# A four-block attention kernel on one core: all of the key spread by transfers, padded query features, and new orders

## The reference, cut to what matters

```python
attn  = softmax(q @ k.T * D**-0.5)                 # block 3, per head
attn2 = softmax(gate * attn)
out   = (w * attn2 + (1 - w) * attn) @ v @ w_proj + b_proj
```

## Time and profile before

| | before |
|---|---|
| median of 3 runs | 479.83 us (478.34 to 479.87) |
| the profiled execution | 478.8 us, span 477.0 us |
| mean granted TensorE clock | 0.989 |
| PE busy | 435.7 us (91%) |
| DVE busy | 405.2 us (85%) |
| ACT busy | 353.5 us (74%) |
| POOL busy | 341.8 us (72%) |
| DMA packets | 33012, 18.26 MB |

### The profile page before, as it was taken

One profiled execution on the slowest core, in us unless ns is written; L12 is line 12 of the kernel. 1 busy time (PEld: TensorE's weight loads), 2 busy tenths in 40 slices (PEclk: granted clock), 3 DMA queues, 4 the chain that ended last, 5 costly groups with the idle time before them and its releaser, 6 DMA issues.

```text
span 477.0 us, 18181 instructions
## 1 busy us (share of the span) xinstructions
PE 435.7 (91%) x7436; PEld 325.4 (68%) x7436; DVE 405.2 (85%) x1208; ACT 353.5 (74%) x765; POOL 341.8 (72%) x548
## 2 busy tenths in 40 slices
PE   3878989999989999998999999999999999888886
PEld 2256767677758686776867776777676867665675
DVE  6476758687999898999998989899998899998975
ACT  2243557758798887988789879897969695978763
POOL 7022556779689779689979796968787978886731
PEclk9979899999999999999999999999999999999999
DMA  6831201102111110130101010200100000000000
GB/s 180 208 82 40 54 20 36 47 18 59 31 25 30 35 43 21 34 101 19 32 23 43 21 28 14 65 21 20 47 19 2 21 2 19 8 12 12 4 12 24
DMA packets 33012, 18.26 MB, mean 38 GB/s; under 512 B 5280, under 2 KB 32800, under 8 KB 32928
## 3 DMA queue, kind: packets, MB, share of 16 engines
q1 hardware_dynamic: 32352, 17.07, 13.7%
q10 hardware_dynamic: 576, 0.02, 0.1%
HBM read 9.74 MB, written 2.10 MB: 25 GB/s over the span
## 4 chain that ended last, share of the span: by engine, by line
PE 39%; POOL 24%; DVE 17%; ACT 12%; issue 4%; DMA 2%; SPq 0%; POOLq 0%; ACTq 0%; DVEq 0%
PE MC L1575 6%; POOL call L439 6%; PE TP L1552 6%; PE FP L1484 5%; POOL call L419 5%; PE MA L1498 4%; PE SP L1543 2%; POOL ft L377 2%; DMA call<-in_ctx 2%; PE FP L1467 2%; PE FP L1471 2%; DVE WT L1028 2%; DVE mx L1071 2%; ACT ffn L720 2%; DVE emn L1090 2%
## 5 line engine op out<-in xcount | busy, mean ns | idle before, releaser
L1575 PEld LDWEIGHTS MC<-Vc,ET 128*64 128x64 f32 x2048 | 65.2, 138 | 17.6 <-issue 8.1
L1552 PE MATMUL TP<-ident,call 128*128 128x128 f32 x512 | 74.6, 278 | 2.8 <-POOL call L439 2.0
L1575 PE MATMUL MC<-Vc,ET 128*64 128x25 f32 x2048 | 71.5, 218 | 4.4 <-DVE n L1108 1.4
L1552 PEld LDWEIGHTS TP<-ident,call 128*128 128x128 f32 x512 | 56.7, 141 | 16.8 <-POOL call L439 5.8
L439 POOL TENSOR_TENSOR call<-call,Gs 128x1024 f32<-128x1024 f32 x32 | 60.9, 1904 | 1.5
L419 POOL TENSOR_TENSOR call<-call,rsh 128x1024 f32<-128x1024 f32 x32 | 60.9, 1905 | 1.4
L377 POOL TENSOR_SCALAR ft<-ft 128x512 f32<-128x512 f32 x64 | 39.9, 623 | 10.1 <-ACT ft L612 5.2
L1028 DVE TENSOR_TENSOR WT<-FP,mask 128x512 f32<-128x512 f32 x64 | 41.8, 681 | 5.9 <-PE FP L1484 5.8
L664 ACT ACTIVATE ET<-TP 128x512 f32<-128x512 f32 x64 | 36.5, 595 | 13.9 <-PE TP L1552 13.5
L1071 DVE TENSOR_REDUCE mx<-SP 128x16 f32<-128x1024 f32 x32 | 38.9, 1214 | 2.4 <-PE SP L1543 2.3
L1484 PEld LDWEIGHTS FP<-ft 32*64 32x64 f32 x2048 | 33.4, 135 | 10.9 <-DVE WT L1028 3.5
(11 more groups left out here) (218 smaller groups left out, 1093.8 us busy)
## 6 DMA issues: line engine op xcount, KB each, us to landing
Cd<-in_ctx SPq DMA_DIRECT2D x32, 128.0 KB, 2.7
call<-in_ctx SPq DMA_DIRECT2D x4, 512.0 KB, 8.2
xall<-in_x SPq DMA_DIRECT2D x4, 512.0 KB, 4.6
cz<-cT SPq DMA_DIRECT2D x64, 32.0 KB, 1.9
cz<-csq SPq DMA_DIRECT2D x64, 32.0 KB, 1.8
kX<-kT SPq DMA_DIRECT2D x128, 8.0 KB
out_x<-X SPq DMA_DIRECT2D x16, 128.0 KB, 1.9
ffn<-in_L_ffn_w_gate SPq DMA_DIRECT2D x1, 256.0 KB, 4.8
```

The source lines that it names most:

```text
L1552: last = pe.transpose(TP[:, c:c + P], src[:, c:c + P], ident[:, :])
L1575: last = mm(MC[64 * j:64 * j + 64, c + 32 * q:c + 32 * q + 25], weights[:, q, 64 * j:64 * j + 64], Vc[g.p][:, 2 * u + j, q, 0:25], start=T ...
```

## The change

1. **No mask products.** `masked` goes from POOL's list (64 instructions), and `spread` issues sixteen transfers per group where it issued eight. `kXd` counts to 256 per buffer. Both `kX` buffers are now cleared whole.
2. **Padded query features.** `Rq2` holds, for w = 0 and w = 1, the query features in 64-row blocks of which the 32 rows of the other strip are zero. The query product of `features` takes K = 64 rows, as the key product behind it does. So w now picks every second strip (`r = 32 * (2 * x + w)`, `ft[:, t, w::2, :]`). `Rq` and `own` lie in what is later the output buffer `X4[0]`.
3. **New orders** on all five engines, with other runs of `zeros` (443 products in place of 359), and a few waits that these orders need or no longer need (`add_X2`, `with_bias`, `less` and `quant_kh` wait for one semaphore more, `attend1` for one fewer).

```diff
                 for x in range(2):
                     for w in range(2):
-                        r = 32 * (2 * w + x)
+                        r = 32 * (2 * x + w)
...
             def spread(g):
                 at(sp, s("kTs"), g.k + 1)
                 at(sp, s("sc"), g.k * 4 - 4)
-                for h in (0, 1, 2, 3, 8, 9, 10, 11):
+                for h in range(H):
                     sp.dma_start(kX[g.p][8 * h:8 * h + 8, h % 8, :, :].rearrange("p b m -> p (b m)"),
...
-            def masked(g):
-
-                at(pool, s("kTs"), g.k + 1)
-                for h in range(4, 8):
-                    pool.tensor_scalar(kX[g.p][:, h, :, :].rearrange("p b m -> p (b m)"), kT[g.p][:, :], bm[:, h:h + 1],
-                                       1.0, ALU.mult, ALU.mult).then_inc(s("kX"), 1)
...
+            for r in range(4):
+                v.memset(Rq2[32 * r:32 * r + 32, 1 - r % 2, :], 0.0).then_inc(s("Rk"), 1)
...
-                v.memset(t[:, 0:4, :, :], 0.0).then_inc(s("kXz"), 1)
+                v.memset(t[:, :, :, :], 0.0).then_inc(s("kXz"), 1)
...
+            for r in range(4):
+                v.tensor_copy(Rq2[32 * r:32 * r + 32, r % 2, :], Rq[32 * r:32 * r + 32, :]).then_inc(s("Rk"), 1)
...
-                    r = 32 * (2 * w + x)
-                    mm(FP[:, 512 * x:512 * x + 256], Rq[r:r + 32, :], qT[r:r + 32, :], start=True, stop=True)
+                    mm(FP[:, 512 * x:512 * x + 256], Rq2[64 * x:64 * x + 64, w, :], qT[64 * x:64 * x + 64, :],
+                       start=True, stop=True)
...
-                    at(pe, s(f"kXd{g.p}"), g.half * 128 + 128)
+                    at(pe, s(f"kXd{g.p}"), g.half * 256 + 256)
...
+            spread(G[4]); load(G[8]); store(G[1]); strips(G[9]); spread(G[5]); load(G[9]); strips(G[10])
+            rows(3); store(G[2]); spread(G[6]); load(G[10]); strips(G[11]); spread(G[7]); store(G[3])
```

More of the change, by code:

```diff
@@ L470, in _ @@
[L470 to L474, removed]
@@ new lines, in _ @@
+            pe.wait_ge(s("n1"), 1); outA(G[0], 1); rows_BT(G[2]); rows_CT(G[1]); zeros(8, TP, 1); queries(G[1])
+            ffn0_in(G[2]); scores(G[1], 0)
+            pe.wait_ge(s("WT"), 14); weights0(G[3], 1)
+            pe.wait_ge(s("thR"), 3); ffn0_out(G[2]); turn2(G[0], 0); turn2(G[0], 1)
+            pe.wait_ge(s("vr"), 3); out0(G[3], 0); out0(G[3], 1)
+            pe.wait_ge(s("n1"), 2); outB(G[0], 0)
+            pe.wait_ge(s("ls"), 3); scores(G[1], 1); turn2(G[0], 2); turn2(G[0], 3); features(G[4], 0)
@@ new lines, in _ @@
+            pe.wait_ge(s("n2"), 3); outB(G[1], 1)
+            pe.wait_ge(s("qiT"), 4); ffn_gu(G[0], 0); turn1(G[2], 1)
+            pe.wait_ge(s("fe"), 22); values(G[3])
+            pe.wait_ge(s("n2"), 4); outA(G[2], 0); project_T(G[1]); rows_BT(G[4])
+            pe.wait_ge(s("hh"), 1); ffn_gu(G[0], 1)
+            pe.wait_ge(s("n1"), 5); project(G[1])
+            pe.wait_ge(s("Vc"), 16); features(G[5], 1); turn2(G[2], 0); ffn0_in(G[4])
+            pe.wait_ge(s("fe"), 24); rows_T(G[6])
+            pe.wait_ge(s("hh"), 2); scores(G[2], 1)
@@ new lines, in _ @@
+            pe.wait_ge(s("n1"), 6); ffn_dn(G[0], 1)
+            pe.wait_ge(s("xqT"), 2); turn1(G[3], 0); turn1(G[3], 1); rows_CT(G[4])
+            pe.wait_ge(s("out"), 2); outB(G[2], 0)
+            pe.wait_ge(s("qiT"), 5); ffn_gu(G[1], 0)
+            pe.wait_ge(s("F"), 13); turn2(G[2], 2); features(G[6], 1)
+            pe.wait_ge(s("n2"), 5); outA(G[3], 0)
+            pe.wait_ge(s("hh"), 3); scores(G[3], 1)
+            pe.wait_ge(s("fe"), 28); values(G[4]); turn2(G[2], 3); rows_T(G[7]); rows_BT(G[5]); turn2(G[3], 0)
@@ new lines, in _ @@
+            pe.wait_ge(s("WT"), 26); weights0(G[6], 1)
+            pe.wait_ge(s("vr"), 6); out0(G[6], 0); scores(G[4], 0); ffn_down(G[1], 1)
+            pe.wait_ge(s("WT"), 28); features(G[7], 0)
+            pe.wait_ge(s("hT"), 4); ffn_in(G[2]); out0(G[6], 1)
+            pe.wait_ge(s("ls"), 9); ffn_gu(G[2], 0); ffn_dn(G[1], 0); turn2(G[3], 2); turn2(G[3], 3)
+            pe.wait_ge(s("out"), 3); ffn_dn(G[1], 1)
+            pe.wait_ge(s("fe"), 30); features(G[7], 1)
+            pe.wait_ge(s("out"), 4); outB(G[3], 1); turn1(G[4], 0)
@@ new lines, in _ @@
+            pe.wait_ge(s("ls"), 11); rows_CT(G[6]); features(G[8], 1)
+            pe.wait_ge(s("qiT"), 7); scores(G[5], 1)
+            pe.wait_ge(s("hT"), 6); turn2(G[4], 2)
+            pe.wait_ge(s("n2"), 9); ffn_dn(G[2], 1); turn2(G[4], 3)
+            pe.wait_ge(s("fe"), 36); values(G[6])
+            pe.wait_ge(s("S"), 19); ffn_in(G[3]); rows_T(G[9])
+            pe.wait_ge(s("out"), 6); outB(G[4], 1)
+            pe.wait_ge(s("xqT"), 4); turn1(G[5], 0); turn1(G[5], 1); rows_BT(G[7])
+            pe.wait_ge(s("ls"), 12); queries(G[6])
@@ new lines, in _ @@
+            pe.wait_ge(s("vr"), 9); out0(G[9], 0); out0(G[9], 1)
+            pe.wait_ge(s("X3"), 6); outA(G[6], 1); features(G[10], 0); turn2(G[6], 1)
+            pe.wait_ge(s("hh"), 10); scores(G[7], 0); turn2(G[6], 2)
+            pe.wait_ge(s("S"), 26); turn2(G[6], 3); features(G[10], 1)
+            pe.wait_ge(s("n1"), 14); outB(G[6], 0)
+            pe.wait_ge(s("S"), 27); ffn_down(G[4], 0)
+            pe.wait_ge(s("ls"), 15); rows_CT(G[8])
+            pe.wait_ge(s("fe"), 44); values(G[8])
@@ L1851, in _ @@
[L1851 to L1853 removed]
+            pe.wait_ge(s("xqT"), 9); project_T(G[9]); ffn0_out(G[12])
+            pe.wait_ge(s("oT"), 10); turn1(G[10], 0)
+            pe.wait_ge(s("out"), 16); project(G[9]); turn1(G[10], 1)
+            pe.wait_ge(s("QT"), 12); ffn_gu(G[8], 0)
+            pe.wait_ge(s("WT"), 54); weights0(G[13], 1)
@@ new lines, in _ @@
+            pe.wait_ge(s("n1"), 24); ffn_dn(G[9], 1); ffn0_in(G[14])
+            pe.wait_ge(s("hh"), 21); ffn_gu(G[10], 1)
+            pe.wait_ge(s("F"), 49); turn2(G[11], 2)
+            pe.wait_ge(s("out"), 20); outA(G[12], 0)
+            pe.wait_ge(s("WT"), 64); values(G[13]); ffn0_out(G[14])
+            pe.wait_ge(s("hh"), 22); scores(G[12], 1)
+            pe.wait_ge(s("vr"), 15); out0(G[15], 0); turn2(G[11], 3); out0(G[15], 1); ffn_down(G[10], 0)
+            outB(G[11], 1); zeros(15, TP, 1)
```

1131 lines of the change are left out of this document (556 added, 575 removed).

## The result

| | before | changed |
|---|---|---|
| median (lowest to highest) of 4 runs each | 479.85 us (478.34 to 480.23) | 490.4 us (489.6 to 493.19) |
| ratio, 95% interval | | 1.0244 [1.0198, 1.0289] |
| profiled execution: span | 477.0 us | 491.2 us |
| mean granted TensorE clock | 0.989 | 0.978 |

The forecast was 475 us, the range 465 to 484. The changed kernel is slower than the slowest rival that the prediction had worked out (484 us). The ratio is the one on record; the two medians of the table alone give 1.022, which lies in its interval.

What follows compares the result with a forecast made beforehand. TensorE was taken to bound the middle, with VectorE close behind and GpSimd's list deciding in some stretches. From 478.8 us, -6.4 - 3.0 + 5.0 + 0.8 = -3.6 gave 475 us, range 465 to 484.

Steps and rivals of the forecast that it cites:

- slowest rival: First score products, released by the last transfer: each of fourteen groups waits 1 us, +14, 484 us; chance 0.21.
- padded features: TensorE's feature calls: first product pair 0.43 us instead of 0.63, 32 times; -6.4 us, bounds 0 and 10.6.
- no mask products: GpSimd's list loses 29.6 us, of which 7.4 us stand on the chain; -3.0 us taken, lower bound 0.
- sixteen transfers: SP's spread grows to 12.6 us, so scores wait where the cover is short; +5.0 us, bounds 0 and +20.
- setup on VectorE: Start of the program: larger clears and four copies, 2.3 us, delay the context copies; +0.8 us, bounds 0 and +2.3.
- zeros: 84 more TensorE products, most in groups 11 to 15 where TensorE must wait anyway; 0, bound +5.8 us.
- the rest of the orders: Added waits of `add_X2`, `with_bias`, `less` and `quant_kh` have a whole group's time as cover; 0.
- Worth nearly its full size in the middle: From 100 to 400 us, TensorE idle 3.6%: shortening its own list gains nearly the full size.
- the gap: Idle 0.33 us before the key products' weight load; a rival had it stay: features term 0, 481.6 us, chance 0.10.

Runs made afterwards that it cites:

- e3: The kernel before with the padded query features alone, its own orders, eight transfers and mask products kept: 476.31 us, ratio 0.9946.
- e12: e1 with the query features unpadded again (K = 32): 487.8 us, ratio 1.0179.
- e6: The kernel before without GpSimd's 64 mask products, nothing in their place: 479.03 us, ratio 0.9998.
- e1: The changed kernel with the spreads of groups 4 to 9 and 13 put ahead of the strips, store or load before them on SyncE: 484.42 us, ratio 1.0109.
- e4: The kernel before with padded features, no mask products and all sixteen transfers, everything but the new orders: 476.85 us, ratio 0.9956.
- e5: e1 without the 68 products with zeros in groups 11 to 14: 486.6 us, ratio 1.0155.
- e9: e1 with half of the transfers, eight of sixteen, so eight heads are missing from the result: 483.53 us, ratio 1.0094.
- e2: The changed kernel with 30 and 48 products with zeros before the first score products of groups 5 and 6: 487.89 us, ratio 1.0187.
- e11: The kernel before with three products with zeros at the head of each of its 32 feature calls: 483.23 us, ratio 1.0102.

## Why the prediction was wrong, step by step

| step | predicted | measured (from) |
|---|---|---|
| padded features | -6.4 | -2.6 (e3), -3.4 (e12, intervals overlap) |
| no mask products | -3.0 | -0.1 (e6) |
| sixteen transfers, behind what stands ahead on SP | +5.0 | +6.5 (changed less e1), and +0.6 (e4 less e3 and e6, not told from nothing) |
| setup on VectorE | +0.8 | not by itself: its copies are inside e3, its wider clears inside e6 |
| zeros | 0 | no gain without 68 of them (e5) |
| the rest of the orders | 0 | +7.3 (e1 less e4), +7.1 (e9 less e3) |
| sum | -3.6 | -2.6 - 0.1 + 6.5 + 0.6 + 7.3 = +11.7 |

The measured sum is no proof of the parts: its terms are differences of ratios that add up to the 1.0244 of the changed kernel.

- **"The rest of the orders: 0"** is the step that failed by most: +7.3 us. I had looked at the waits that the change adds and at the covers of one product, and took the rearranged lists for a wash. The added waits do cost next to nothing, 1.5 us of GpSimd's idle time in e1; what wasn't priced is the order itself. I had no way to price it from the trace of before, so the range should have held some per cent either way. Which calls make the 7 us stays open.
- **"Worth nearly its full size in the middle"** failed too. TensorE at 96% was read as the bound; the chain had it at 39%. The shorter products came out as forecast, 6.3 us by pitch, and less than half of that arrived. That the two pitches together met the 1.06 us was partly luck: the first pair takes 0.54 where 0.43 was forecast, the second 0.53 where 0.63 to 0.7 was to stay (with 0.7 the text's own sum is 1.13). The Trainium skill's rule (page "TensorE: Matmul & The Clock Gate", Part 3, "The mechanism", in its list of what overlaps; the same section also lets a load go ahead into a background weight buffer) that the loads must go to another group of rows to overlap would have left the gap; the trace after disagrees: the key weights start to load at 233.54, 0.22 us before their products, while the query products over the same 64 rows still run.
- **Mask products.** The four pieces on the chain were an upper bound of 7.4 us, and the value was the lower bound, 0, as far as can be told (e6). GpSimd's pieces on a chain say where it was last, not by how much.
- **Sixteen transfers.** The size was near by luck, the shape was not as forecast. The waits, 5.0 us together, stand in groups 5 and 6 alone (1.93 and 3.08), not as tenths in groups 2 to 6; the sum itself had counted 2.1, 1.6 and 2.3 for groups 4 to 6. And the 6.5 us of e1 hold the fall of the granted clock too. For the spread's start I had counted on about 2 us of strips still running when the keys were ready; it was 4.2 us of strips in group 5, and 3.8 in group 6, where the rows of x and a store stand behind the strips. The latter was the condition that the slower rival named, but waits came in two groups, not fourteen. The fall of the granted clock after each wait, some 2.7 us (e2), wasn't priced at all.
- **Setup.** The 2.3 us came from the mean of two unlike copies, of 0.86 and 0.28 us; the four new ones took 1.15 together, and the copy of the context starts no later.

## What to carry to other kernels

In a kernel of several in-order lists that wait for each other, the busiest engine isn't the bound by that alone: of some 6 us taken from TensorE less than half arrived (e3), of some 6 us added three quarters or more (e11), of 29 us taken from GpSimd nothing that can be told (e6). Ask for each term who is late next. Time the parts of a change and its new order apart: here the parts alone give 2 us, and the order takes 14. Before a long burst goes onto a queue, read what stands ahead of it there, and move the urgent burst in front of what has slack.

## What was not expected of the hardware

One wait of 3.08 us was followed by nearly 10 us at a mean granted clock of 0.53, and one of 1.93 us by a window at 0.83; products with zeros in the same waits kept it at 1.00 (e2). In e1 an idle 0.95 us was followed by 0.74 over 5 us. 68 products with zeros, 4.7 us of work without a result by count, made a kernel no slower, and without them the clock fell to 0.90 over 35 us (e5).
